# A macaron block on one core: routed down in three fp16 products, two norms' sums on ScalarE, the bias add on VectorE, stores and fills issued by ScalarE, and a new plan

## What is computed

```python
x = x + 0.5 * ffn(layernorm(x))
x = x + attn(layernorm(x))
x = x + 0.5 * ffn(layernorm(x))

def ffn(x):                         # 8 experts of 128 hidden units, 2 of them per token; shared hidden 256
    shared = (silu(x @ ws_gate.T) * (x @ ws_up.T)) @ ws_down.T
    scores = sigmoid(x @ gate_weight.T)
    w, idx = top_k(scores, 2);  w = 2.5 * w / w.sum(-1)
    routed = sum over the two experts e of  w[e] * ((silu(x @ w_gate[e].T) * (x @ w_up[e].T)) @ w_down[e].T)
    return shared + routed

def attn(x):                        # xx is x shifted by one token
    k, v, r = proj(mix(x, xx))      # three projections 256 -> 256
    state_t = k_t * v_t + exp(time_decay) * state_(t-1)
    out = r * (time_first * k * v + state)
    return (layernorm(out) * ln_g + ln_b) @ Wo.T
```

## Time and profile before

| | |
|---|---|
| time, median of 3 runs (lowest to highest) | 1095.18 us (1091.2 to 1098.09) |
| the profiled execution's own time | 1096.77 us |
| its span, first to last instruction | 1095.0 us |
| mean granted clock of TensorE, as a share of full speed | 0.946 |

### The profile page before, as it was taken

One profiled execution on the slowest core, in us unless ns is written; L12 is line 12 of the kernel. 1 busy time (PEld: TensorE's weight loads), 2 busy tenths in 40 slices (PEclk: granted clock), 3 DMA queues, 4 the chain that ended last, 5 costly groups with the idle time before them and its releaser, 6 DMA issues.

```text
span 1095.0 us, 23262 instructions
## 1 busy us (share of the span) xinstructions
PE 916.0 (84%) x7488; PEld 661.1 (60%) x7488; DVE 798.9 (73%) x2485; ACT 408.7 (37%) x737; POOL 700.3 (64%) x684
## 2 busy tenths in 40 slices
PE   1858979798889989999999989999999888969750
PEld 0526747665558567676457766567666676756640
DVE  5968655386788888899999769998987743736442
ACT  5433432344425343444443433536343323133210
POOL 2666726776787855477787668553738763665565
PEclk9979989998999999999999999999999988989885
DMA  7988979998877965466337975745335998999994
GB/s 221 273 216 187 204 179 198 204 217 201 199 191 169 209 143 144 112 159 141 102 118 163 199 189 127 160 122 121 96 94 111 243 250 219 221 226 304 196 288 134
DMA packets 337989, 198.58 MB, mean 181 GB/s; under 512 B 251728, under 2 KB 319952, under 8 KB 337872
## 3 DMA queue, kind: packets, MB, share of 16 engines
q1 hardware_dynamic: 312432, 129.84, 50.7%
q0 software_dynamic: 24576, 67.14, 24.4%
q10 hardware_dynamic: 864, 0.12, 0.1%
HBM read 47.05 MB, written 92.27 MB: 127 GB/s over the span
## 4 chain that ended last, share of the span: by engine, by line
SPq 30%; issue 16%; PE 14%; POOL 14%; DVE 13%; DMA 8%; ACT 3%; POOLq 0%; ACTq 0%; DVEq 0%
SPq L755 18%; SPq L728 7%; PE ps L1032 5%; POOL y_got L855 4%; POOL xsA L838 3%; POOL xsB L838 3%; PE ps L965 2%; SPq L763 2%; DMA y_got<-ysB,y_pos 2%; DVE acc L1257 2%; DMA xt<-rows 2%; SPq L749 2%; DVE stat L1271 2%; DMA y_got<-ysA,y_pos 2%; POOL p_exp L829 2%
## 5 line engine op out<-in xcount | busy, mean ns | idle before, releaser
L925 PE MATMUL ps<-xq,w_hi 128*128 128x128 f16 x1248 | 225.0, 225 | 37.7 <-DMA xq<-xsB 27.7
L927 PE MATMUL ps<-xq,w_hi 128*128 128x128 f16 x1248 | 225.0, 225 | 0.0
L929 PE MATMUL ps<-xq,w_lo 128*128 128x128 f16 x1248 | 224.9, 225 | 0.0
L1257 DVE SCALAR_TENSOR_TENSOR acc<-y_got,share,acc 128x256 f32<-128x256 f32 x256 | 129.9, 511 | 81.5 <-DMA y_got<-ysB,y_pos 58.8
L838 POOL DMA_INDIRECT xsB<-rows,pos x128 | 136.6, 1067 | 68.4 <-issue 34.2
L855 POOL DMA_INDIRECT y_got<-ysB,y_pos x128 | 126.8, 991 | 76.1 <-issue 38.2
L965 PE MATMUL ps<-wd,hid 128*128 x624 | 154.4, 390 | 13.1 <-ACT y_sb L1149 6.0
L855 POOL DMA_INDIRECT y_got<-ysA,y_pos x128 | 131.9, 1030 | 51.1 <-issue 43.4
L838 POOL DMA_INDIRECT xsA<-rows,pos x128 | 131.0, 1023 | 48.4 <-issue 35.9
L925 PEld LDWEIGHTS ps<-xq,w_hi 128*128 x1248 | 126.3, 101 | 47.5 <-DMA xq<-xsB 30.7
L1230 DVE SCALAR_TENSOR_TENSOR hid<-ps,hid 128x512 f32<-128x512 f32 (+1 forms) x144 | 96.6, 678 | 73.2 <-PE ps L929 49.7
(11 more groups left out here) (138 smaller groups left out, 1778.0 us busy)
## 6 DMA issues: line engine op xcount, KB each, us to landing
ysA<-y_sb SPq DMA_DIRECT2D x36, 512.0 KB, 3.8
ysB<-y_sb SPq DMA_DIRECT2D x36, 512.0 KB, 4.4
acc<-in_x_dram SPq DMA_DIRECT2D x16, 512.0 KB, 4.8
out_dram<-acc SPq DMA_DIRECT2D x16, 512.0 KB
xsA<-zeros SPq DMA_DIRECT2D x36, 128.0 KB
xsB<-zeros SPq DMA_DIRECT2D x36, 128.0 KB
acc<-in_w_chunks_dram SPq DMA_DIRECT2D x10, 256.0 KB, 5.1
xq<-xsA SPq DMA_TRANSPOSE x156
```

The source lines that it names most:

```text
L925: nc.tensor.matmul(half, w_hi[2 * k + b][:, cols], hi, start=(j == 0 and k == 0), stop=False, skip_group_check=True)
L927: nc.tensor.matmul(half, w_hi[2 * k + b][:, cols], lo, start=False, stop=False, skip_group_check=True)
L929: mm = nc.tensor.matmul(half, w_lo[2 * k + b][:, cols], hi, start=False, stop=(j == many - 1 and k == KC - 1), skip_group_check=True)
L1257: v.scalar_tensor_tensor(out=acc[:, s, h, :], in0=y_got[:, h, k, :], scalar=share[:, s, h, k:k + 1], in1=acc[:, s, h, :], op0=ALU.mult, op ...
```

## The change

- **Routed down.** It runs as the shared one does: the weights are split once into `wd_hi` and `wd_lo` (scaled by 256, the evacuation scales back), each quad's hidden tile into halves, and each block has three fp16 products where it had one in fp32. `hidden_hi` and `hidden_lo` run for every chunk; `hid` has 3 buffers (4 before) and is free after `hidden_lo`, the halves have 3 sets (2 before).
- **Norms 1 and 3.** `sums` on ScalarE replaces `stats` on VectorE: four passes with an accumulated sum, the mean, four passes of squares about the mean with an accumulated sum, and the variance. Both kinds of pass write to `norm32`, so that buffer is taken by `sums` and no longer by `norm`.
- **Bias.** The same add stands on VectorE.
- **Issues.** `y_store` and `tails` are in ScalarE's list. SyncE keeps loads, both kinds of transposes and the stores of the output.
- **Plan.** New costs for what changed, new constants, and a table `SHIFT` with an offset for every single task; the urgency is the formula plus both offsets.

```diff
-N_ROWS, N_XT, N_XQ, N_Y, N_HID, N_SPLIT = 3, 2, 4, 3, 4, 2
+N_ROWS, N_XT, N_XQ, N_Y, N_HID, N_SPLIT = 3, 2, 4, 3, 3, 3
...
-        plan.add(engine, name, key, us, urgency + LATER.get(kind, 0.0), *after, **more)
+        plan.add(engine, name, key, us, urgency + LATER.get(kind, 0.0) + next(shift[name]), *after, **more)
...
     def moments(n, s, at, after):
+        if n != "2":
+            add("act", "sums", (n, s), 4.2, at, after + [("rstd", (n, s - 1)) if s else None],
+                not_before=at - 5 if n == "1" and group_of("A", s) >= 2 else 0.0)
+            add("pool", "rstd", (n, s), 1.62, at + 2, [("sums", (n, s)), ("norm", (n, s - 1)) if s else None])
+            return
...
-        if what == "S":
-            add("act", "hidden_hi", key, 0.63, at + 3, [("gated", key)])
...
+        add("act", "hidden_hi", key, 0.63, at + 3, [("gated", key)])
+        add("dve", "hidden_lo", key, 0.72, at + 4, [("hidden_hi", key)])
+        add("pe", "down", key, 1.47 if what == "S" else 0.33 * blocks_of(f, a, b), at + 5, [("hidden_lo", key)])
...
-        add("sp", "tails", (f, g), 5.2, at - 17, [("table", (f, g))], lag=2.0)
+        add("act", "tails", (f, g), 5.2, at - 17, [("table", (f, g))], lag=2.0)
...
-            add("sp", "y_store", (f, g, q), 0.6, at + gap * q + 9, [("evac", key)], lag=3.6)
+            add("act", "y_store", (f, g, q), 0.65, at + gap * q + 9, [("evac", key)], lag=3.6)
...
-        add("pool", "bias", (s,), 2.66, at + 8, [("norm", ("2", s)), ("o_bias_out", ())])
+        add("dve", "bias", (s,), 1.2, at + 8, [("norm", ("2", s)), ("o_bias_out", ())])
...
-                        cols = bass.ds(expert_cols[key][j], P)
-                        mm = nc.tensor.matmul(half, hid[:, b, tok], wd[:, :, cols], start=(j % 2 == 0),
-                                              stop=(j % 2 == 1 or j == many - 1), skip_group_check=True)
+                        cols, w, w_rest = bass.ds(expert_cols[key][j], P), wd_hi, wd_lo
+                    nc.tensor.matmul(half, hid_h[:, n, tok], w[:, :, cols], start=(first and j % 2 == 0),
+                                     stop=False, skip_group_check=True)
+                    nc.tensor.matmul(half, hid_l[:, n, tok], w[:, :, cols], start=False, stop=False,
+                                     skip_group_check=True)
+                    mm = nc.tensor.matmul(half, hid_h[:, n, tok], w_rest[:, :, cols], start=False,
+                                          stop=(last and (j % 2 == 1 or j == many - 1)), skip_group_check=True)
...
+            def sums(n, s):
+                if n == "1":
+                    act.wait_ge(x_in[s % 4], 16 * (s // 4 + 1))
+                else:
+                    act.wait_ge(out_resid_done, val("out_resid", s, per=NT))
...
+                for j in range(NT):
+                    ins = nc.scalar.activation(norm32[:, j, :], acc[:, s, j, :], ACT.Copy,
+                                               accum_out=sum_x[n][:, j:j + 1])
+                ins.then_inc(summed[n], 1)
+                act.wait_ge(summed[n], s + 1)
+                nc.scalar.activation(less_mean[n][:], sum_x[n][:], ACT.Copy, scale=-1.0 / C).then_inc(centre_done[n], 1)
+                act.wait_ge(centre_done[n], s + 1)
+                for j in range(NT):
+                    ins = nc.scalar.activation(norm32[:, j, :], acc[:, s, j, :], ACT.Square,
+                                               bias=less_mean[n][:, j:j + 1], accum_out=sum_sq[n][:, j:j + 1])
+                ins.then_inc(squared[n], 1)
+                act.wait_ge(squared[n], s + 1)
+                nc.scalar.activation(var_eps[n][:], sum_sq[n][:], ACT.Identity, bias=eps[:], scale=1.0 / C)\
+                    .then_inc(var_done[n], 1)
```

More of the change, by code:

```diff
@@ new lines, in schedule @@
+    shift = {name: iter(row) for name, row in SHIFT.items()}
+    def add(engine, name, key, us, urgency, *after, **more):
+        kind = name + key[0] if name in ("gate_up", "down", "gather", "fetch", "silu", "gated", "norm", "stats", "sums") and isinstance(key[0], str) else name
+        plan.add(engine, name, key, us, urgency + LATER.get(kind, 0.0) + next(shift[name]), *after, **more)
+    PACE = 34.2
+    FIRST_A = 44.9
+    FIRST_T = 107.1
+    A_LEAD = 248.4
+    A_GAP = 33.6
+    E_LEAD = 46.5
@@ L400, in takes @@
             return (("bank", uses[name]),)
-        if name == "norm" and key[0] != "2":
+        if name == "sums":
             return (("norm", 1),)
@@ L438, in frees @@
         if name == "row_lo":
[L439 removed]
+            gone(("sums", ("1" if key[0] == "A" else "3", key[1])), "norm", 0)
         elif name == "scatter":
@@ L443, in frees @@
             gone(("fetch", key[1:]), "xq", 0)
-        elif name == "hidden_lo" or name == "down" and key[0] == "E":
+        elif name == "hidden_lo":
             gone(("silu", key), "hid", 0)
@@ L489, in program @@
     chunk_no = {key: i for i, key in enumerate(chunks)}
-    shared = [key for key in chunks if key[0] == "S"]
-    shared_no = {key: i for i, key in enumerate(shared)}
     quads = list(streams["quads"])
@@ new lines, in y_store, with tails @@
+            def y_store(f, g, q):
+                n = quad_no[f, g, q]
+                act.wait_ge(evac_done, val("evac", "E", f, g, q, per=2))
+                many = blocks_of(f, g, q)
+                act.dma_start(ys[f, g][4 * q * P:(4 * q + many) * P, :].rearrange("(j p) c -> p j c", p=P),
+                             y_sb[:, n % N_Y, 0:many]).then_inc(y_stored[n % N_Y], 16)
+            def tails(f, g):
+                act.wait_ge(table_done, val("table", f, g))
+                to = xs[f, g]
+                at = nc.values_load_multi_w_load_instructions(
+                    tail_at[0:1, :], engines=[mybir.EngineType.Activation], min_val=0, max_val=NE * REGION - P,
+                    skip_runtime_bounds_check_because="counts are at most the group's tokens")[1]
+                for e in range(NE):
+                    act.dma_start(to[bass.ds(at[e], P), :], zeros[:]).then_inc(tails_in, 16)
+                act.dma_start(to[NE * REGION:NE * REGION + P, :], zeros[:]).then_inc(tails_in, 16)
```

297 lines of the change are left out of this document (190 added, 107 removed), and 116 rows, old and new, of the table SHIFT.

## The result

The changed kernel takes 1089.98 us in the median of 15 runs (1074.88 to 1095.65) against 1095.18. The ratio, 0.9883 (0.9853 to 0.9912), or 1.2% and 13 us, is made from the eight faster of these runs, and the profiled execution (1094.21 us, span 1092.4) is one of the seven slower ones, so what follows reads stretches and waits from that profile, while savings are worked out from ratios. 0.9883 of 1095 is 1082 us, and each run of the changed kernel with an edit is set against that. The mean of all 15 runs is 1087.7, only 8 us under the 1095.6 of the kernel before; against it each such run would gain some 5 us more or lose 5 less. Either way it is not the 48 that the sum gave.

A forecast was written before the change was run, and what follows sets the result against it. Bound: compute in the middle, SyncE's issue at both ends. From 1096.8 us, -24 - 20 - 7 + 5 + 9 - 11 = -48 gives 1048.8, 1047 against the median; range 1003 to 1096, the forecast's own 1031 to 1066.

The forecast's parts named there:

- the 48 that the sum gave: Whole kernel: all terms of the prediction added up to 48 us saved, 1047 us against the median.
- the ends: Stretches 60 to 315 and 838 to 1048 us, on both sides of the mixer, read as bound by SyncE's issue.
- SyncE's queue, -44: Both ends: stores and fills leaving SyncE's queue save 24 us in the first and 20 in the second.
- its rival: Both ends: the DMA engines hold them, so moving issues saves nothing; 1102 us, chance 0.12.
- TensorE in the middle, -7: From 315 to 838 us: fp16 down products save 13 us of TensorE, of which half was counted.
- VectorE in the middle, +18 to 475: From 315 to 838 us: VectorE gains 18 us of work; as a rival it takes over, 1072 us, chance 0.08.
- ScalarE, 5.0 us a sum: Norms 1 and 3: each of 32 sums takes 5.0 us on ScalarE, 160 in all.
- the 327 forecast: From 315 to 838 us: ScalarE's load of 327 of 523 us, covered by its idle time unless its queue blocks.
- expose the halves: Rival at routed down: ScalarE's queue order makes it wait for its halves, up to 1.31 us a quad; 1143 us, chance 0.12.
- First rows, +5: Start of the kernel: norm32, held from the sums on, makes the first rows later, costing 5 us.
- A longer way to routed down, +9: Routed down: waiting for high and low halves costs 0.11 us for each of 80 quads, 9 us.
- The plan, -11: Both ends: the new order fills a third of TensorE's 33 us of remaining idle time, saving 11 us.

The follow-up runs named there:

- e13: The kernel before, its order kept, with 68 transposes fewer on SyncE's queue: 1060.02 us, ratio 0.9657.
- e17: The kernel before with 68 transposes fewer, each replaced by four copies of 128 bytes on SyncE's queue: 1115.22 us, ratio 1.0199.
- e6: The changed kernel in its own order, only the 80 y stores and eight fills put back on SyncE: 1112.85 us, ratio 1.0179.
- e1: The kernel before in its own order, only the 80 y stores and eight zero fills moved from SyncE to ScalarE: 1104.38 us, ratio 1.0076.
- e9: The changed kernel, order kept, with one of routed down's three products left out: 1082.26 us, ratio 0.9898.
- e14: The kernel before, order kept, routed gate and up without the weights' remainder product for half the channels: 1094.62 us, ratio 0.9998.
- e15: The changed kernel, order kept, with the bias cut to one column after the first sequence: 1083.46 us, ratio 0.988.
- e18: The kernel before with its order, only the bias add moved from GpSimd to VectorE: 1087.9 us, ratio 0.9944.
- e7: The changed kernel in its own order, only the bias add put back on GpSimd: 1106.5 us, ratio 1.0128.

## Why the prediction was right and wrong

The direction was right and the size was not. The step that failed: it counted the time freed on SyncE's queue in the ends one for one, -44, and let the new order fill idle time there on top, -11. The runs showed instead that one us of this queue is worth about half a us of the time (0.43 and 0.51), and that in the changed kernel the freed time came out as waits of the same queue, 138 us in the two ends against 7.

**SyncE's queue, -44.** The mechanism was right: issue time on this queue counts, and the DMA load does not (e13, e17). The size was wrong. I counted the time freed in the ends one for one because the queue had no waits there. One us of it is worth 0.43 to 0.51 in the kernel before. The whole kernel has about 80 x 0.58 + 8 x 5 = 86 us of stores and fills; at 0.43 that is 37, an estimate, and undoing the move in the new order cost 32 (e6). So the move by itself was worth some 32 to 37, not 44. That it can't be had without a new order (e1, +8) the prediction didn't say.

The Trainium skill (page "DMA: Bandwidth & Descriptors", section "Issuing engines are not separate DMA queues") says that a second issuing engine saves only the sequencer's time, usually small beside the DMA; the prediction took that as nothing for its rival. What was saved is indeed queue time, but here it is not small: with the same relief of the DMA engines, the time went 59 us up with the queue's.

**TensorE in the middle, -7.** Mis-sized; it measured nothing, twice (e9, e14). The busy share of 94% misled: over the whole span TensorE's idle time grew by 10 to 22 of the 24.5 us that it saved.

**VectorE in the middle, +18 to 475.** The bias measured 1.218 us, as the subtraction's row had it. But the middle has 427.0 us of VectorE, not 475, while the second end, where the new order put projections, has 140.2 instead of 112.4; and e15 shows no worth. That rival falls. I gave GpSimd's relief no term of its own; the bias alone gains 6 us in the old order.

**ScalarE, 5.0 us a sum.** It is 4.4, from the first pass to the end of the variance:

```profile
5.38 0.40 ACT L1369 ACTIVATE norm<-acc 128x256 f32<-128x256 f32 x1
5.68 0.19 ACT L1369 ACTIVATION_READ_ACCUMULATOR norm<-acc 128x1 f32 x1
...
9.44 0.30 ACT L1380 ACTIVATE var_eps<-sum_sq,eps 128x4 f32<-128x4 f32 x1
```

ScalarE has 297.3 us busy in the middle. Of the 327 forecast some 29 were issues, which busy time leaves out, so 298 came true, partly by luck: 15 sums of 4.4 lie there, not 12 of 5.0. Its queue did not expose the halves, but what the prediction named in passing does show: around each of the eight fills ScalarE stands still for 4.5 to 9.2 us. What that costs was not tested.

**First rows, +5.** The first fetch starts at 81.3 us instead of 76.2: 5.1 later. That the whole kernel ends later by as much is not shown.

**A longer way to routed down, +9.** It measured nothing; TensorE's waits for the low half are this one row, for routed and shared together:

```profile
PE ps L1167 <- DVE hid_l L1487: 2.3, 1, 2.3
```

**The plan, -11.** I let the new order fill idle time in the ends on top of the relief. It did take work off the queue there: besides some 48 us of issues, 48 of the 247 transposes, 61 us at 1.28 each, 109 together. But the queue's waits in the ends grew by 131 us, and TensorE did a little less there than before (211.1 and 169.5 us against 214.9 and 172.9). What came into the ends was projections, 120 of 384 where 48 had been. The order also had another task: the edits in the old order cost 8.7%, and it first had to take that back.

With -32 for the issues (e6) and -6 for the bias (e18), the gain of 13 leaves about +25 for sums, halves and order together, where the prediction had -4 (-7, +5, +9 and -11). That difference comes from values measured under different orders, so it is a remainder and no measurement; with the 27 us that the bias is worth in the new order (e7) it would be +46. Which part of it is the sums', the halves' or the order's stays open: it would take orders planned with equal care for each set of edits. The down product put back into fp32 under the new order was not tried.

## What to carry to other kernels

A queue without waits that carries the chain is a bound, but not one for one: ask what becomes due next, and price the queue by taking work off it with the order kept (here 0.43 us for one, while the engine with 84% busy time was worth nothing). An edit that adds work to an in-order queue is hard to judge under an order made for other tasks: issues and sums looked like a loss in both directions here. When two queues hold a kernel in turn, relief of one shows up as waits on it.

## What the runs showed of the hardware

- A pass on ScalarE with a sum costs two records: 0.40 us for 128x256 (Square with a bias 0.49) and a read of the accumulator of 188 ns (changed kernel) that overlaps it in part, so that passes start 0.40 and 0.49 us apart.
- A copy of 128 bytes with an address from a register took 228 ns of issue in the median, but some 0.43 us of the queue each (116 us for 272, e17), a third of a transpose of 128 KB (1.28).
- The issue of the same store of 512 KB took 0.37 us in the median on ScalarE's queue (changed kernel) and 0.58 on SyncE's (before).
